# Cross-attention, block attention and experts on one core: products of the keys in parts, values earlier, and the experts' sums and turned rows in another order

## What is computed

```
x = x + xattn(layernorm(x), ctx, ctx)        # 8 sequences of 512 rows, 512 wide; 77 context rows each; 16 heads
h = layernorm(x)
h1 = h_ln1_attention(h) + h                  # grouped attention: 16 query heads, 4 key heads; over the 8 sequences
z = layernorm2(h1)                           # 4096 rows
probs = softmax(z @ router)                  # 8 experts, the best two of each row
expert e takes at most 1280 of its rows:     # gelu(z @ w1[e]) @ w2[e], times the share
x = x + h1 + sum of the experts' rows
```

## Time and profile before

| | us |
|---|---|
| median of 3 timed runs | 1589.51 (1587.81 to 1590.07) |
| profiled execution, whole | 1583.6 |
| its span | 1581.8 |
| TensorE busy | 1477.9 |
| VectorE, ScalarE, GpSimd busy | 920.4, 712.1, 833.5 |
| mean granted clock of TensorE | 0.976 of full |

### The profile page before, as it was taken

The page is one execution under the profiler, slowest core; times in us unless marked ns, Lnnn a source line. Parts: engine busy times, 40 slices in busy tenths (PEclk is TensorE's granted clock), DMA queues, the critical chain, the costliest instruction groups (busy, mean ns, idle before and its releaser), DMA issues. The chain is left out here.

```text
span 1581.8 us, 31078 instructions
## 1 busy us (share of the span) xinstructions
PE 1477.9 (93%) x11056; PEld 1309.9 (83%) x11057; DVE 920.4 (58%) x1741; ACT 712.1 (45%) x1425; POOL 833.5 (53%) x951
## 2 busy tenths in 40 slices
PE   8798899999999999899859998999999899999986
PEld 6577788888888888788749988998999789899876
DVE  3767677777778767788665464433233653453361
ACT  2445545555555555565415453433233643342341
POOL 2445455556666556698725566542542855354332
PEclk9999999999999999999959999999999999999999
DMA  7212211122222111222223343432422534333222
GB/s 262 66 63 75 88 59 50 63 72 82 75 75 67 62 66 64 75 93 88 99 80 91 78 88 100 104 83 54 107 58 48 135 90 103 81 94 54 32 35 25
DMA packets 64400, 125.96 MB, mean 80 GB/s; under 512 B 13369, under 2 KB 13785, under 8 KB 63724
## 3 DMA queue, kind: packets, MB, share of 16 engines
q1 hardware_dynamic: 45932, 93.81, 18.2%
q0 software_dynamic: 17920, 29.31, 10.9%
q10 hardware_dynamic: 384, 0.61, 0.1%
HBM read 89.14 MB, written 46.27 MB: 86 GB/s over the span
## 5 line engine op out<-in xcount | busy, mean ns | idle before, releaser
L1503 PEld LDWEIGHTS hidden_ps<-gT,w 128*128 128x128 f32 x2880 | 350.3, 192 | 11.3 <-ACT hT L1408 3.9
L1503 PE MATMUL hidden_ps<-gT,w 128*128 128x256 f32 x2880 | 352.9, 284 | 7.0 <-ACT hT L1408 3.5
L1530 PE MATMUL expert_ps<-w,hT 128*128 128x512 f32 x1440 | 341.0, 396 | 8.1 <-DVE og L1458 8.1
L1530 PEld LDWEIGHTS expert_ps<-w,hT 128*128 128x128 f32 x1440 | 271.9, 191 | 65.9 <-DVE og L1458 8.9
L1283 POOL TENSOR_TENSOR w<-raw,w 128x1024 fp32r<-128x1024 f32 x62 | 152.9, 2514 | 261.5 <-ACT w L1277 261.5
L1433 DVE TENSOR_TENSOR hT<-gl,hT 128x512 fp32r<-128x512 f32 x160 | 125.9, 795 | 249.0 <-ACT hT L1408 225.3
L1406 ACT ACTIVATE gl<-hidden_ps 128x512 f32<-128x512 f32 x160 | 95.7, 598 | 326.6 <-PE hidden_ps L1503 258.6
L1387 POOL DMA_INDIRECT out_dram<-og,idx x78 | 126.0, 1616 | 72.8 <-DVE og L1458 44.0
L1458 DVE TENSOR_SCALAR og<-expert_ps,kept 128x512 f32<-128x512 f32 x80 | 59.3, 749 | 156.4 <-PE expert_ps L1530 147.4
L1416 ACT ACTIVATE gT<-yk 128x256 fp32r<-128x256 f32 x160 | 67.0, 419 | 127.7 <-DVE yk L1444 118.7
L1375 POOL DMA_INDIRECT xg<-normed_tokens,idx x78 | 86.4, 1108 | 56.2 <-POOL idx L1370 30.9
(11 more groups left out here) (184 smaller groups left out, 3079.5 us busy)
## 6 DMA issues: line engine op xcount, KB each, us to landing
raw<-L_ffn_moe_w_dram SPq DMA_DIRECT2D x64, 512.0 KB
normed_tokens<-h SPq DMA_DIRECT2D x128, 65.0 KB
xa<-x_dram SPq DMA_DIRECT2D x32, 256.0 KB, 2.7
xc<-x_dram SPq DMA_DIRECT2D x32, 256.0 KB, 3.0
attended_rows<-x SPq DMA_DIRECT2D x32, 256.0 KB, 2.1
fx<-attended_rows SPq DMA_DIRECT2D x128, 64.0 KB
out_dram<-fx SPq DMA_DIRECT2D x128, 64.0 KB
fx<-qkv_rows_dram SPq DMA_DIRECT2D x1, 1536.0 KB, 6.7
```

The costliest lines, as they stand in the source:

```text
L1503: last = pe.matmul(pH[:, q, f * W:(f + 1) * W], w1[p][l][:, k, cols], xT[g.s % 2][r][:, k, :], start=k == 0 and n == 0, stop=k == KT - 1 a ...
L1530: last = pe.matmul(pY[:, k, :], hT[par][l][:, f, k * P:(k + 1) * P], w2[p][r][:, f, :], start=f == 0 and n == 0, stop=f == FT - 1 and n == 2)
```

## The change

The change has eight parts. The first six are in the block stage, the last two in the expert stage.

1. The keys are computed in three passes from high and low parts. ACT writes the high parts of context and key weights, DVE the low parts, in the space of `wqkv` and `wpj`; the block weights are then split in the other order (`wpj` first).
2. The value parts move: parts 0 and 1 in step 2 (ahead of q and behind it), 2 in step 3, 3 in step 4 ahead of everything, 4 in step 4. SP starts their spreading DMAs one step behind the step of the product, after its loads.
3. q's banks are taken as soon as half of the shifted scores is read (`bank_free`).
4. In odd steps 5 to 13 ACT copies `pt` ahead of `xt`, and DVE subtracts xT's low part behind the sums of the shares.
5. In steps up to 38 DVE's reduction and reciprocal of the second attention (L985, L986) stand behind the turn of q (L992).
6. `choose` for the last tiles stands at the end of step 49 in place of the beginning of 50, and piece 7 of the first expert's weights is subtracted by POOL in the expert stage in place of DVE in step 50.
7. TensorE turns gathered rows (i-4) behind the second products (i-7).
8. DVE makes the sums `og` (i-7) ahead of the gathered rows (i-4).

```diff
-LATE_LOW = {LATE + 11: 6, LATE + 12: 7}
+LATE_LOW = {LATE + 11: 6}
+VALUES = {2: ((0, 0), (1, 2)), 3: ((2, 2),), 4: ((3, -1), (4, 2))}
+VALUE_BANKS = (4, 5, 4, 6, 5)
-CHOICES = {STEPS - 7: (0, 26, 0), STEPS - 6: (0, 26, 1), STEPS - 5: (0, 26, 2), STEPS - 2: (26, 31, None)}
+CHOICES = {STEPS - 7: (0, 26, 0), STEPS - 6: (0, 26, 1), STEPS - 5: (0, 26, 2), STEPS - 3: (26, 31, None)}
...
             for old, t_old, j_old in ousted[kind, t, j]:
-                pe.wait_ge(*read_out[old](t_old, j_old))
+                if old == "s" and kind != "s" and place[kind, t, j] < 2:
+                    pe.wait_ge(s["shifted"], 2 * t_old + 1)
+                else:
+                    pe.wait_ge(*read_out[old](t_old, j_old))
...
@@ SP, step i, now behind load_x and the load of xc @@
+                for b, _ in VALUES.get(i - 1, ()):
                     sp.wait_ge(s["val_done"], b + 1)
...
@@ ACT, ahead of the first steps @@
+            for k in range(KT):
+                act.wait_ge(keys_in[k], 32)
+                act.activation(cTh[0][:, k, :], cT[:, k, :], ACT.Copy)
+                act.activation(wpj[0][:, k, :], rk[:, k, :], ACT.Copy).then_inc(s["key_hi"], 1)
...
@@ ACT, step i @@
+                turned_first = i % 2 == 1 and LP <= i <= FF
...
@@ DVE, ahead of the first steps @@
-            for t in range(2):
-                stats_x(t)
+            for k in range(KT):
+                dve.wait_ge(s["key_hi"], k + 1)
+                dve.tensor_tensor(cTh[1][:, k, :], cT[:, k, :], cTh[0][:, k, :].bitcast(F32), ALU.subtract)
+                dve.tensor_tensor(wpj[1][:, k, :], rk[:, k, :], wpj[0][:, k, :].bitcast(F32), ALU.subtract)\
+                   .then_inc(s["key_lo"], 1)
+                if k % 2 == 1:
+                    stats_x(k // 2)
...
@@ PE, the keys @@
-                pe.wait_ge(keys_in[k], 32)
-                for n in range(8):
-                    last = pe.matmul(bank("key", n)[:, 0:HC], rk[:, k, m * P:(m + 1) * P], cT[:, k, h * HC:(h + 1) * HC],
-                                     start=k == 0, stop=k == KT - 1)
+                pe.wait_ge(s["key_hi"], k + 1)
+                for n_pass, (w, c) in enumerate(PASSES):
+                    if n_pass == 1:
+                        pe.wait_ge(s["key_lo"], k + 1)
+                    for n in range(8):
+                        last = pe.matmul(bank("key", n)[:, 0:HC], wpj[w][:, k, m * P:(m + 1) * P],
+                                         cTh[c][:, k, h * HC:(h + 1) * HC], start=k == 0 and n_pass == 0, stop=final)
...
@@ POOL, experts @@
+                if isinstance(c, int) and c == 0 and i == 5:
+                    low(pool, 0, 0, CH - 1)
...
@@ DVE, experts, step i @@
+                g = At(c, i - 7, PER)
+                if g.within(NG):
+                    for k in range(GB):
+                        dve.wait_ge(s["fc2_mm"], g.count(GB, k + 1))
+                        need(dve, scattered[k], g.count(16))
+                        dve.wait_ge(s["share_kept"], g.count(1, 1))
+                        dve.tensor_scalar(og[:, k, :], pY[:, k, :], kept[:, g.s, k:k + 1], None, ALU.mult)\
+                           .then_inc(s["summed"], 1)
                 g = At(c, i - 4, PER)
...
-                g = At(c, i - 7, PER)
-                if g.within(NG):
-                    for k in range(GB):
...
@@ PE, experts, step i: around the second products @@
-                if not (isinstance(c, int) and c == 0 and i == 5):
-                    turn_rows(c, i)
                 g = At(c, i - 7, PER)
...
+                if not (isinstance(c, int) and c == 0 and i == 5):
+                    turn_rows(c, i)
```

More of the change, by code:

```diff
@@ L182, in psum_jobs, with values @@
     fz, fq, fs, fo, ft, fr = (tile(i, FF + n) for n in range(6))
-    jobs = [("xt", tx, 0, 1)] + [("pt", tp, j, 0) for j in range(4)] + [("p2t", fo, 0, 0)]
+    def values(stage):
+        return [("val", b, 0, 1) for b, at in VALUES.get(i, ()) if at == stage]
+    jobs = values(-1) + [("xt", tx, 0, 1)] + [("pt", tp, j, 0) for j in range(4)] + [("p2t", fo, 0, 0)]
+    jobs += values(0)
     if i % 2 == 0:
@@ L622, in _ @@
             for i in range(STEPS):
[L623 to L628, removed]
+                turned_first = i % 2 == 1 and LP <= i <= FF
+                if not turned_first:
+                    normed_high(i)
                 if i == 2:
@@ L981, in _ @@
                 f = tile(i, FF + 2)
-                if f is not None:
+                if f is not None and i > LATE:
                     dve.wait_ge(s["exp2"], f + 1)
@@ L992, in _ @@
                     dve.transpose(hq, parts(bank("qkv", f, 0))).then_inc(s["q_turned"], 1)
+                f = tile(i, FF + 2)
+                if f is not None and i <= LATE:
+                    dve.wait_ge(s["exp2"], f + 1)
+                    need(dve, s["shared2"], f - 1)
+                    chained(dve.tensor_reduce(den2[:, :], p2, X, ALU.add))
+                    dve.reciprocal(rec2[:, f % 2, :], den2[:, :]).then_inc(s["rec2_done"], 1)
+                f = tile(i, FF + 1)
+                if f is not None:
                     dve.wait_ge(s["v_kept"], f + 1)
@@ L1009, in _ @@
                     stats_f(i)
+                if i in CHOICES and i >= STEPS - 3:
+                    choose(*CHOICES[i])
                 if i <= FF:
@@ L1012, in _ @@
                         sooner(i + 1)
-                    later(i + 1)
+                    if i % 2 == 1 or not LP <= i + 1 <= FF:
+                        later(i + 1)
                 t = tile(i, -1)
@@ L1045, in turn_z, with values @@
                 transposes("zt", f, z).then_inc(s["zt_mm"], 1)
+            def values(i, stage):
+                for b, at in VALUES.get(i, ()):
+                    if at == stage:
+                        pe.wait_ge(wv_in, 16)
+                        bank_free(pe, "val", b)
+                        n = min(P, S * SK - P * b)
+                        for k in range(KT):
+                            last = pe.matmul(bank("val", b)[0:n, :], cT[:, k, P * b:P * b + n], rv[:, k, :],
+                                             start=k == 0, stop=k == KT - 1)
+                        last.then_inc(s["val_mm"], 1)
             def count_places(a, b, batches):
@@ L1129, in _ @@
                     count_places(*COUNTS[i])
-                b = i - 2
-                if 0 <= b < VB:
-                    pe.wait_ge(wv_in, 16)
-                    bank_free(pe, "val", b)
-                    n = min(P, S * SK - P * b)
-                    for k in range(KT):
-                        last = pe.matmul(bank("val", b)[0:n, :], cT[:, k, P * b:P * b + n], rv[:, k, :],
-                                         start=k == 0, stop=k == KT - 1)
-                    last.then_inc(s["val_mm"], 1)
+                values(i, 2)
                 if tq is not None:
```

56 lines of the change are left out of this document (32 added, 24 removed).

## The result

| | before | changed |
|---|---|---|
| median, us | 1588.66 (4 runs, 1586.90 to 1590.07) | 1646.16 (4 runs, 1645.83 to 1647.59) |
| profiled execution: span, us | 1581.8 | 1644.2 |
| TensorE busy, us | 1477.9 | 1493.8 |
| mean granted clock | 0.976 | 0.952 |

The ratio is 1.0366, 95% interval 1.0353 to 1.0379: 57.5 us slower. I had predicted 1626, with a range of 1600 to 1650. Sign and mechanism came out as forecast. The time lies 20 us above the likeliest value: the block stage gave back nothing, where I had put 17 us, and the first expert step lost 5 us, where I had put nothing. The profiled execution of the kernel before was quicker (1583.6 us) than its timed runs in the table, so differences between the two profiles come out some 5 us larger than those between medians.

What follows compares the result with a forecast made beforehand. TensorE bounds the kernel (busy 1477.9 of 1581.8 us), through its work, idle time and clock. Experts +54 and block stage -17 gave +37 on the 1589.5 median: 1626 us, range 1600 to 1650.

Steps and rivals of the forecast that it cites:

- The ring: Expert stage: gathered rows, low pieces, gather, scatter, landing, og close a one-step ring, turns 19 to 22 us; +54 us.
- Rival 1: Expert stage: the ring doesn't bind (turn below about 13 us), the swap only removes waits; 1562 us; chance 0.09.
- rival 2: Expert stage: the ring binds but with landings of 3.3 us; +38 - 17, 1610 us; chance 0.14.
- Rival 3: Expert stage: a turn with two pieces exceeds 23.4 us, some 20 full steps pay 1 us; 1650 us; chance 0.11.
- The signs: New profile: second products wait 7 to 15 us each for og near 940, 980, 1300, 1410; TensorE busy near 1475.
- What the swap wins: Expert stage: removed waits for yk (4.03 and 6.40 us), without the ring worth 10.4 us and the clock.
- The landing: Scatter's landing in the experts: 5.5 us kept from the trace; by the skill's price some 17 us less time.
- (a): Block stage, steps of 284 to 592 us: TensorE's pv no longer waits 0.60 us for L992; -9.1 us.
- (b): End of block stage: low piece and choose no longer stand ahead of the last maximum; -2.7 us.
- (c): Block stage, steps 4 to 13: half of TensorE's 10.0 us of waits for pT goes; -5 us (0 to -10).
- (d): Block stage, keys in short format: end near 20.4 in place of 24.0; with (e) 0 us (-4 to +6).
- (e): Block stage, early values: second scores near 50, TensorE idles 5 us, later repaid; with (d) 0 us (-4 to +6).

Runs made afterwards that it cites:

- e5: The changed kernel, both expert orders kept, with GpSimd's scatter a step sooner (group i-7 in place of i-8); 1600.2 us, ratio 1.0094.
- e1: The changed kernel with VectorE's sums og put back behind the gathered rows, TensorE's new order kept; 1646.38 us, ratio 1.0375.
- e8: The kernel before with only VectorE's reduction and reciprocal of the second attention behind its turn of q, in steps up to 38; 1579.31 us, ratio 0.9951.
- e6: The changed kernel with both expert orders put back and the value parts one a step in steps 2 to 6, behind q; 1577.43 us, ratio 0.9939.
- e7: The changed kernel with both expert orders put back and SyncE starting the spreading DMAs ahead of its load of x; 1577.85 us, ratio 0.9935.
- e13: e6 with e11's increments, and GpSimd beginning piece 7 of the low weights only after VectorE's last low gathered half of group 0; 1572.45 us, ratio 0.9904.
- e9: e6 with piece 7 of the first expert's low weights subtracted by VectorE in step 50 again; 1576.69 us, ratio 0.9921.
- e11: e9 with 64 increments of an unread semaphore on TensorE ahead of the keys; 1573.82 us, ratio 0.9906.

## Why the prediction was right, and where it failed

- **The ring.** Right in place and size. Turns of 22.1 us with two low pieces measured 21.9. The turns of 19.2 and 19.4 us stand behind scatters with less to write (0.42 and 0.00 MB for 0.89); I took 1.5 us off for that, and the trace has 2.5 to 2.7. To group 10 I had +23, measured +19.9. Full steps cost nothing, as I had it (23.4 us in both kernels), but the loop's start at group 14 cost most of the 5.2 us between groups 10 and 19: 3.5 us of gaps for 0.9, and first products of 14.5 us for 11.75, at a granted clock of 0.50 from 1118 to 1121 us. To group 25 I had another +28, measured +31.7 since group 19, of which 2.1 is again a longer gap at the loop's start (2.83 for 0.76 us). Group 28 cost nothing where I had 5, the end -0.4 in place of +2. The experts behind their first step sum to +56.5; +54 was forecast. About 9 of the 56.5 are the loop's gaps and the slow products behind them, which the forecast didn't have, so the ring itself is nearer 48, and part of the good fit is luck.
- **The rivals.** Rival 1 (the ring doesn't bind; its "rows 4" should read rows 5) and rival 2 (landings of 3.3 us) fall with the traces. Rival 3's premise came true: VectorE's subtractions for `hT` fell beside GpSimd's pieces and took 1.12 us on average for 0.79, 52 of the 61 us that VectorE is busier. But its effect did not come, for full steps had room for it.
- **The signs.** Three of the four long waits for `og` came (8.1, 13.9 and 13.2 us, near 945, 980 and 1308). None came near 1410, and the fourth long wait is for `yk` (13.2 near 1272). TensorE's busy time was to stay near 1475 and is 1493.8, for I counted the lower clock in one place only.
- **What the swap wins.** Wrong. I wrote that without the ring the removed waits for `yk` would be worth 10.4 us and the clock. e5 has the ring open and pays 4.4; e1 has no ring and pays 51, by a second chain (turned rows, gathered rows, `og`, second products) that I had not looked for because I walked the two moves only together.
- **The landing.** The prediction says that the price of the Trainium skill (DMA: Bandwidth & Descriptors, Anatomy of one DMA, SWDGE path), which it makes 1.3 us less a turn, would give 17 us less. By its own walks that is too much: 2.2 us less a turn gave 16, 0.9 gave 9, so 1.3 gives some 10. The measured landings (5.1 and 5.4 us from issue) side with the earlier trace rows.
- **(a)** -9.1 forecast, -9.4 in the ledger, -8.6 alone (e8). Right.
- **(b)** -2.7 forecast; -0.8 at the first turned rows, which single traces can't tell from nothing (e8, without this part, has +1.8 over the same stretch), then +5.1 at the piece's new place. I costed a piece on GpSimd at its own time and not beside VectorE's subtractions.
- **(c)** -5 forecast (0 to -10), -1.1 measured over tiles 4 to 13 (the same in e6): the waits for `pT` were 10.0 and are 8.6 us. I had halved a list entry without following one instance.
- **(d), (e)** 0 forecast (-4 to +6), +12.1 measured. This is the step that did most to move the time off the forecast, and the piece of (b) is the other. I had named the chain (bias sum of part 1, DMA of part 0, SyncE's load, TensorE's turning) and put the second scores near 50 (53.6). Then I let the time of two values, done early, pay for it. It pays only when nothing waits (e7, 8 us back). In the changed kernel the same wait comes again at the last part (12.5 of the 28.8 us), where transposed shares wait 5.7 us for the bank. The keys ended at 22.0, not 20.4: their first 8 products took 2.42 us where later 8 take 1.28. The granted clock is full there (1.00 from 5 to 11 us), so why stays open. Part 0's product, ahead of q, took 5.37 us where 3.60 is usual, and there the granted clock is low (0.82 from 26 to 29 us, 0.61 from 29 to 32).
- The sum: block stage +0.8 for -17 (whose lower end, -24, should be -26 by its own terms), first expert step +5.1 for 0, the rest +56.5 for +54, in all 62.4 for 37 between the profiled executions, 57.5 between the medians.

## What to carry to other kernels

When an instruction that waits for a DMA moves ahead of the work that, through other engines, leads to that DMA's issue, add up the ring: it sets a floor under every step, and steps with little work pay for it. Test each of two moves alone, for they can hide each other's cost (here +51 and +70 us alone, +50 together). A DMA queue that starts transfers in program order is a list like any engine's: put what another engine waits for ahead of loads that wait themselves (18 us here for one move).

## What was not expected of the hardware

- **Two engines' subtractions exclude each other.** VectorE's low gathered half, two operands in SBUF, ended 0.6 us behind GpSimd's in place of after 0.42 us. Three subtractions for `hT` spanned 4.49 us beside two low pieces, where one alone takes 0.69. The Trainium skill (SBUF — State Buffer, two separate sides) says that VectorE, when it reads two operands in SBUF, and GpSimd share a port pair as an exclusive lock held for a whole instruction; the rows here and e13 agree.
- **The position of a loop's code costs time.** TensorE's gaps at the loop's start were 3.9 us in sum in e9 and 1.6 in e11 with 64 increments ahead. The changed kernel's are 6.4 for 1.7 before, and e11 doesn't show how much of that is the position. The Trainium skill (Runtime: NRT & Kernel Launch, Instruction fetch mechanics) says that a taken branch whose target is not in the window held has to fetch it; that the gaps are such fetches is only my guess, and no row here shows a fetch.
- **A scatter with no valid row lands sooner.** In the changed kernel the two halves of an empty group's scatter (issued at 948.71 and 950.63, 0.00 MB moved) released `og` 2.9 and 2.8 us after their issue. Those issued at 968.04 and 969.97 (0.89 MB) took 5.1 and 5.4.
